# Half-height score products, one hidden pair moved into the round before, and a causal mask split in three, in a two-layer recurrent kernel

## The reference

```python
xn = _layernorm(x)
s = _L0_attn_ref(xn, ...)          # tanh mixes, r k v w g, wkv6, group norm, W_o
g = _silu(_L0_ffn_ref(xn, ...))    # silu(gate)*up, 2-of-4 sparsity, down
x = x + s * g
xn = _layernorm(x)
s = _L1_attn_ref(xn, ...)          # _ssd, below, times silu(res), w_out
g = _silu(_L1_ffn_ref(xn, ...))
x = x + s * g
```

```python
L = jnp.where(tri, jnp.exp(cs[..., :, None] - cs[..., None, :]), 0.0)
scores = jnp.einsum('znid,znjd->znij', Cc, Bc) * L
y_diag = jnp.einsum('znij,znjh->znih', scores, Xc)
```

## Time and profile before

| | us |
|---|---|
| median of 3 runs (lowest, highest) | 735.85 (734.74, 736.4) |
| the profiled execution | 735.66 |
| its span, first to last instruction | 733.9 |
| TensorE busy in the span (matmuls) | 711.3 (97%) |
| VectorE, ScalarE, GpSimd busy | 497.5, 342.0, 77.2 |
| chain that ended last: TensorE, VectorE, issue | 76%, 12%, 5% |

### The profile page before, as it was taken

The page is one execution under the profiler, slowest core; times in us unless marked ns, Lnnn a source line. Parts: engine busy times, 40 slices in busy tenths (PEclk is TensorE's granted clock), DMA queues, the critical chain, the costliest instruction groups (busy, mean ns, idle before and its releaser), DMA issues.

```text
span 733.9 us, 17949 instructions
## 1 busy us (share of the span) xinstructions
PE 711.3 (97%) x6896; PEld 590.1 (80%) x6896; DVE 497.5 (68%) x1207; ACT 342.0 (47%) x678; POOL 77.2 (11%) x85
## 2 busy tenths in 40 slices
PE   5998999999999999999999999999999999999998
PEld 3777688877888688886888868888788878888686
DVE  4976599547895478955787558855689547895133
ACT  1411685226832468215762168522584236821690
POOL 6301011101011010100111001110101101011020
PEclk9989999999999999999999999999999999999999
DMA  7900351125400353013531145102540136301360
GB/s 238 404 23 29 102 88 32 15 73 144 75 2 15 88 146 59 2 28 104 117 59 16 30 138 95 32 15 69 142 80 3 15 87 145 59 2 26 119 116 16
DMA packets 122444, 55.93 MB, mean 76 GB/s; under 512 B 104384, under 2 KB 114176, under 8 KB 120832
## 3 DMA queue, kind: packets, MB, share of 16 engines
q1 hardware_dynamic: 122368, 54.76, 30.3%
HBM read 42.35 MB, written 12.40 MB: 75 GB/s over the span
## 4 chain that ended last, share of the span: by engine, by line
PE 76%; DVE 12%; issue 5%; DMA 2%; SPq 2%; ACT 2%; POOL 1%; DVEq 0%; ACTq 0%; POOLq 0%
PE psum L1486 58%; PE psum L1707 2%; PE psum L1722 2%; PE psum L1514 2%; PE psum L1565 1%; PE psum L1760 1%; PE psum L1931 1%; PE psum L1595 1%; PE psum L1733 1%; DVE beats L1085 1%; PE psum L1577 1%; DVE own L992 1%; PE psum L1554 1%; PE psum L1873 1%; SPq L453 1%
## 5 line engine op out<-in xcount | busy, mean ns | idle before, releaser
L602 ACT ACTIVATE BC<-psum 64x256 f32<-64x256 f32 x128 | 81.4, 636 | 3.0 <-PE psum L1486 1.3
L1486 PE MATMUL psum<-xn1T,sb_n_gate 128*128 128x256 f32 x256 | 61.3, 382 | 0.0
L1486 PE MATMUL psum<-xn1T,sb_n_up 128*128 128x256 f32 x256 | 60.6, 380 | 0.4 <-DVE cs_row L1294 0.4
L1486 PE MATMUL psum<-xnT,sb_f_gate 128*128 128x256 f32 x240 | 58.5, 386 | 0.0
L1486 PE MATMUL psum<-xnT,sb_f_up 128*128 128x256 f32 x240 | 57.6, 382 | 0.0
L733 ACT ACTIVATE thFB<-psum 128x512 f32<-128x512 f32 x8 | 4.8, 597 | 104.9 <-PE psum L1486 104.9
L1486 PEld LDWEIGHTS psum<-xn1T,sb_n_up 128*128 128x128 f32 x256 | 48.0, 190 | 6.9 <-DVE cs_row L1294 0.8
L1486 PEld LDWEIGHTS psum<-xn1T,sb_n_gate 128*128 128x128 f32 x256 | 48.0, 190 | 6.8
L1486 PEld LDWEIGHTS psum<-xnT,sb_f_up 128*128 128x128 f32 x240 | 44.8, 190 | 6.4 <-issue 0.3
L1486 PEld LDWEIGHTS psum<-xnT,sb_f_gate 128*128 128x128 f32 x240 | 44.2, 189 | 6.8 <-issue 0.2
L1486 PE MATMUL psum<-sb_f_down,hid 128*128 128x256 f32 x224 | 49.5, 379 | 0.0
(11 more groups left out here) (257 smaller groups left out, 1459.0 us busy)
## 6 DMA issues: line engine op xcount, KB each, us to landing
cs_row<-cs_dram SPq DMA_DIRECT2D x8, 1024.0 KB, 4.9
x_dram<-gate SPq DMA_DIRECT2D x8, 512.0 KB, 2.8
cs_half<-cs_dram SPq DMA_DIRECT2D x16, 256.0 KB, 5.9
hidB<-x_dram SPq DMA_DIRECT2D x8, 512.0 KB, 5.9
b_dram<-B_turned SPq DMA_DIRECT2D x32, 128.0 KB, 3.3
hidB<-b_dram SPq DMA_DIRECT2D x8, 512.0 KB, 4.2
X<-in_x SPq DMA_DIRECT2D x9, 256.0 KB, 3.5
XT<-in_x_turned SPq DMA_DIRECT2D x8, 256.0 KB, 3.6
```

The costliest lines, as they stand in the source:

```text
L602: ins = a_.activation(cols[:, par, 2 * pair:2 * pair + 2, :], src[64 * par:64 * par + 64, :, s, :], ACT.Identity)
L1486: ins = t_.matmul(ps(t, name)[first_row:first_row + rows, col:col + n], w, x, start=(k == 0), stop=(k == len(ws) - 1))
```

## The change

1. **Scores by 64 keys.** Each product of 128 keys with 128 queries becomes two of 64 keys: the first 64 keys with all 128 queries, the last 64 keys with the last 64 queries. They stand in the two column halves of the array and swap sides from chunk to chunk. The keys of odd chunks thus lie with their halves exchanged, so `cs_pos`, `Xrow` and `Brow` are loaded by three DMAs each (`KEY_ROWS`).
2. **Mask in three.** Even chunks, odd chunks, and the lower 64 partitions of the odd chunks have a select each, one behind the other; where there is a tile a they wait for `lev_ready` 4, the last of the four `level_next` before `own_taken`.
3. **Pair 1 at the end of the round before**, behind pair 0, in other banks; `th` is filled there by silu (`next_gates`), `hidden_p(a, 1)` stands behind `hidden_p(a, 0)`, and all of `compare(0)` before `mix_g_scaled`.
4. **Order elsewhere.** `end_args` behind `B_by_block`, `gate_tanh` behind `L_exps(0)`, `res0` before `gate_in`; in round 0 the down product is cut up around `keys_turned` and `chunk_states`, the fillers become 4 and 9 products of 128 columns and the last one goes; in round 8 the first B product stands before `carries`.

```diff
+KEY_ROWS = [(slice(0, P), 0, slice(0, P)), (slice(0, 64), 1, slice(64, P)), (slice(64, P), 1, slice(0, 64))]
...
-            return name not in ("p0", "p1", "p2") or (name == "p2" and t.first) or (name == "p0" and not t.first)
+            return name not in ("p0", "p1", "p2") or t.first == (name == "p2")
...
-                    sp_.dma_start(Brow.rearrange("p q c d -> p (q c) d"),
-                                  b_dram.rearrange("(c p d) -> p c d", p=P, d=SD)).then_inc(B_rows, 16)
+                    keys = b_dram.rearrange("(c two p d) -> p c two d", two=2, p=P, d=SD)
+                    for to, r, from_ in KEY_ROWS:
+                        sp_.dma_start(Brow.rearrange("p q (c two) d -> p (q c) two d", two=2)[to, :, r, :],
+                                      keys[from_, :, r, :]).then_inc(B_rows, 16)
...
-                    g.affine_select(out=cs_row[:, :, :], in_=cs_row[:, :, :], compare_op=ALU.is_ge, fill=NEG, base=0,
-                                    pattern=[[0, NQ * SCH], [1, P]], channel_multiplier=-1).then_inc(cs_masked, 1)
+                    if a:
+                        pool.wait_ge(lev_ready, a.count(6, 4))
+                        pool.sem_inc(passed, 1)
+
+                    by_two = cs_row[:, :, :].rearrange("p (c two) q -> p c two q", two=2)
+                    for last, r, two, base in ((P, slice(0, P), 0, 0), (P, slice(0, P), 1, 64), (64, slice(0, 64), 1, -64)):
+                        m = by_two[r, :, two, :]
+                        ins = g.affine_select(out=m, in_=m, compare_op=ALU.is_ge, fill=NEG, base=base,
+                                              pattern=[[0, NQ * SCH // 2], [1, P]], channel_multiplier=-1)
+                        if last == P:
+                            did(ins)
+                    ins.then_inc(cs_masked, 1)
...
-                    for s in range(NQ):
-                        r = half_rows(s)
-                        ins[s] = t_.matmul(ps(t, names[s])[:, i * P:(i + 1) * P], Bf[r, c * P:(c + 1) * P],
-                                           Cf[r, c * P:(c + 1) * P], start=True, stop=True)
+                    for first in range(2):
+
+                        k, at = slice(c * P + 64 * first, c * P + 64 * first + 64), 64 * (first ^ (c % 2))
+                        for s in range(NQ):
+                            r = half_rows(s)
+                            ins[s] = t_.matmul(ps(t, names[s])[at:at + 64, i * P + 64 * first:(i + 1) * P], Bf[r, k],
+                                               Cf[r, c * P + 64 * first:(c + 1) * P], start=True, stop=True)
...
-                    kept_at_work("p2u", 1)
+                    kept_at_work("p2u", 4)
...
-                    down_part(a, 0, 0, 4)
+                    down_part(a, 0, 0, 2)
+                    keys_turned()
+                    down_part(a, 0, 2, 4)
+                    chunk_states()
+                    down_part(a, 1, 0, 2)
                     outputs()
-                    down_part(a, 1, 0, 4)
-                    kept_at_work("yT", 1)
+                    down_part(a, 1, 2, 4)
+                    kept_at_work("yT", 9)
...
-                    kept_at_work("xT1", 6)
+                    ffn_p(a.next(), 1)
```

More of the change, by code:

```diff
@@ L103, in place @@
         b = BANK[name]
-        return b, self.count(PER[b], NTH[name] + EXTRA[b])
+        behind = 2 if name in ("p1g", "p1u") else 0
+        return b, self.count(PER[b], NTH[name] + EXTRA[b] - behind * PER[b])
     def at(self):
@@ L427, in one @@
                     sp_.sem_inc(passed, 1)
-                    wait(X_rows, b.count(16, 16))
+                    wait(X_rows, b.count(48, 16))
                     sp_.dma_start(x_dram.rearrange("(q p n) -> p q n", q=NQ, p=P), Xnat).then_inc(X_stored, 16)
@@ L432, in one @@
                     sp_.sem_inc(passed, 1)
-                    wait(cs_loaded, b.count(48, 16))
+                    wait(cs_loaded, b.count(80, 16))
                     wait(cs_rows_loaded, b.count(16, 16))
@@ L444, in one @@
                     wait(X_stored, b.count(16, 32))
-                    sp_.dma_start(Xrow.rearrange("p q c d -> p (q c) d"),
-                                  x_dram.rearrange("(c p d) -> p c d", p=P, d=SD)).then_inc(X_rows, 16)
-                    wait(B_rows, b.count(16, 16))
+                    keys = x_dram.rearrange("(c two p d) -> p c two d", two=2, p=P, d=SD)
+                    for to, r, from_ in KEY_ROWS:
+                        sp_.dma_start(Xrow.rearrange("p q (c two) d -> p (q c) two d", two=2)[to, :, r, :],
+                                      keys[from_, :, r, :]).then_inc(X_rows, 16)
+                    wait(B_rows, b.count(48, 16))
                     wait(B_blocks, b.count(2, 2))
@@ L733, in ffn_tanh_1, with next_gates @@
                     free(a_.activation(thFB[:, :], ps(b, "F1")[:, :], ACT.Silu, scale=0.5), b, "F1")
+                def next_gates():
+                    for n in range(2):
+                        ffn_tanh(a.next(), f"p{n}", th[n], None)
+                    exp_tables()
                 def exp_tables():
@@ L782, in one @@
                     ffn_tanh_1()
+                    if a.reg is not None:
+                        next_gates()
                 elif a:
@@ L898, in hidden @@
                     return
-                dve.wait_ge(ready, t.count(2, n + 1 if t.first else n))
+                dve.wait_ge(ready, n + 1 if t.first else t.count(1, 2))
                 free(d.scalar_tensor_tensor(out=buf[:, :], in0=buf[:, :], scalar=1.0, in1=ps(t, name + "g")[:, :],
@@ L1124, in differences, with rank_inputs @@
                 did(d.tensor_tensor(dxT[:, :, :], xnT[:, :, 0:T], xnT[:, :, 1:T + 1], ALU.subtract))
+            def rank_inputs(t):
                 after()
@@ L1334, in one @@
                     hidden_p(a, 0)
+                    hidden_p(a, 1)
                     mix_scaled(a, "w")
@@ L1357, in one @@
                     own_taken(a)
-                    end_args()
                     B_by_block(0)
                     B_by_block(1)
+                    end_args()
                     level_next(a, 4)
@@ L1397, in one @@
                     differences(a.next())
+                    rank_inputs(a.next())
                     result()
@@ L1465, in _ @@
             differences(Tile(None, 0, first=True))
+            rank_inputs(Tile(None, 0, first=True))
             rounds(dve, one)
@@ L1902, in kept_at_work @@
                     for _ in range(count):
-                        t_.matmul(ps(a, name)[:, 0:C], ident[:, :], W["f_gate"][:, 0:C], start=True, stop=True)
+                        t_.matmul(ps(a, name)[:, 0:P], ident[:, :], W["f_gate"][:, 0:P], start=True, stop=True)
                 def turned_1():
@@ L1975, in one @@
                     low_levels(a)
+                    ssd_proj(b, "res0", "w_res", 0)
                     gate_in()
-                    ssd_proj(b, "res0", "w_res", 0)
                     ssd_proj(b, "res1", "w_res", 1)
@@ L2069, in one @@
                     X1()
+                    ssd_proj(b, "B0", "w_B", 0)
                     carries()
-                    for name, w in (("B", "w_B"), ("C", "w_C")):
-                        for half in range(2):
-                            ssd_proj(b, f"{name}{half}", w, half)
+                    ssd_proj(b, "B1", "w_B", 1)
+                    for half in range(2):
+                        ssd_proj(b, f"C{half}", "w_C", half)
                     ffn_n(b, 0)
```

49 lines of the change are left out of this document (22 added, 27 removed).

## The result

| | before | changed |
|---|---|---|
| median of 5 runs (lowest, highest), us | 735.15 (734.74, 736.4) | 739.99 (737.96, 741.55) |
| ratio, 95% interval | | 1.0068 (1.0049 to 1.0088) |
| the profiled execution, its span | 735.66, 733.9 | 741.55, 739.8 |
| mean clock in the profiled execution | 0.995 | 0.998 |

The change makes the kernel slower by 0.7%. I had forecast 725.5, faster, with 0.08 for slower; both the sign and the size are wrong. The profiled execution is the slowest of the five: TensorE's clock fell in its round 5. Three of the others have a mean clock of 1.0 and take 737.96 to 739.99.

The account below looks back on a forecast made before the run. The prediction took TensorE's stream, busy 91.60 of 92.00 us in a steady stretch, as the bound. From 735.66 us, -2.8 - 4.1 - 0.6 - 3.4 + 0.8 = -10.1 gave 725.5 us, range 722.5 to 732.0.

Parts of the forecast that it names:

- 0.08 for slower: Whole kernel: the chance given to the change making it slower, against 0.88 for faster and 0.04 for same.
- My part on pair 1: Steady rounds: 3.55 us only moved, costing nothing; between rounds 0 and 1 a gain, -3.55 - 0.6 = -4.1 us.
- the mask's term: Before the high levels: mask behind level 4 makes them later, net 0.2 us a round, bounds -0.2 and +0.5.
- My slower rival: Mask: each select costs what the whole one does, 2.6 us later a round, 744 us; chance 0.05.
- Scores: Scores by 64 keys: 1.48 us instead of 1.99, saving 0.51 us a round.
- the fixed cost: Rival on the scores: a cost per product eats most of the 0.51 us, 728.5 us; chance 0.06.
- quarters in turn: Rival on the scores: array quarters don't run side by side, 3.0 us instead of 1.48, 736 us; chance 0.04.
- the mask's move in round 1: Round 1: the mask no longer blocks a VectorE comparison, a gain of some 0.6 us, between 0 and 1.8.
- The forecast clock: Round 0: longer first filler keeps TensorE's clock up, worth 3.4 us; rival that it falls, 729 us, chance 0.30.
- my 0.6 for the cut-up down product: Round 0: the pieces fill earlier waits, so the chain behind the outputs comes 0.6 us sooner.
- +0.8: Round 8: the end hangs on Brow, whose added DMA issues make it 0.8 us later, bounds 0 and 3.
- What I said would make it wrong: A steady round not about 0.3 us shorter, or a gain of rounds 0 and 1 under 4 us.

Follow-up runs that it names:

- e1: The changed kernel with TensorE's loop beginning at the first slot of a 16 KB instruction block (head_slot 0): 730.9 us, ratio to before 0.9939.
- e7: The kernel before with TensorE's loop at the first slot of a block (head_slot 0), nothing else: 731.94 us, ratio 0.9978.
- e6: The kernel before with only the scores by 64 keys, the mask in three selects and end_args behind the transposes: 738.83 us, ratio 1.0055.
- e13: The kernel before with the loop at the first slot and the three edits of VectorE's order from e12: 730.17 us, ratio 0.9947.
- e2: The kernel before with TensorE's loop at slot 220 of 256 (head_slot 220): 744.79 us, ratio 1.0154.
- e12: e1 with low_taken before level 6's copies, e8's smaller select, and decayed_scores(0) and states_0 (rounds 1 to 7) and round 8's scores before B_decayed: 719.94 us.
- e3: A run with the hint; the text given states neither its kernel nor its time.
- e4: The changed kernel with GpSimd's three selects no longer waiting for level 4: 762.2 us, ratio 1.0389.
- e14: The kernel of e12 with TensorE's loop left where the changed kernel has it: 733.88 us, ratio 0.9985.
- e9: The changed kernel with TensorE's loop at slot 205 of 256 (head_slot 205): 732.66 us, ratio 0.9964.
- e8: e1 with the second select cut to the 64 partitions and 64 queries that need it: 727.56 us, ratio 0.9902.

## Why the prediction was wrong

My sum was -10.1, measured were +5.9 in the profiled execution. Of the 16 us between them, 14.7 lie in rounds 2 to 6.

- **The step that failed first: what is done to the code in front of the loop costs a steady round nothing.** My part on pair 1 said that in a steady round its 3.55 us "are only moved" and "I cost it at nothing". It followed the moved products' waits, but not their instructions: round 0 has more code in front of the loop, and that shifts the loop in its blocks. It cost 8.9 us of pauses, some 1.7 of clock in round 5 and 0.5 before the rounds' first product. No rival named it; none of my views of the kernel before showed it, since there was no pause there, but the profile's line of instruction packets and the branch back were both to be seen.
- **It is not all of it.** With the pause gone a steady round of e1 is still 0.6 us longer than that of its control e7, where I had forecast 0.3 shorter. Most of these 0.9 us is the mask's term, next; the rest I can't split.
- **Mask: the mechanism was right, the term mis-sized.** I had net +0.2 a round, bounds -0.2 and +0.5, and measured +0.81 in round 3, 0.7 to 0.8 in the others. The selects took 1.1 us each, as I said. Two other sizes were off. The starts: I gave the mask 3.4 us behind level 4's last copy, with 0.1 for the two waits between the selects; it took 276.33 - 272.46 = 3.87, since 0.6 us went by before and between the selects. So level 5 was late by 0.70 and not by 0.4. The slack: I counted the 0.39 us from the banks' freeing to the high levels before (283.89 to 284.28) as slack, and let TensorE start 0.2 us behind the freeing. With TensorE waiting there it starts 281.62 - 281.18 = 0.44 us behind it, so there was none. My slower rival had each select cost 2.0 us; the selects did not (1.09), so it was right only in where the lateness goes, to the high levels.
- **Scores: right.** 1.48 forecast, 1.50 measured; the rivals of the fixed cost and of quarters in turn are out.
- **Pair 1: the size was right, the round wrong.** I booked -3.55 in round 1. But round 1 makes pair 1 for round 2 at its own end; the one that falls away is round 7's. Put there, my sum has -5.5 for rounds 0 and 1 and -3.05 for 7 and 8; measured were -4.4 and -2.9. The wait of 0.67 us in round 1 went as forecast. Of the 0.6 for the mask's move in round 1 nearly 0.5 came: its way from the low to the high levels was 10.14 us against 9.46 in round 3, and is 10.50 against 10.28.
- **Round 0.** The forecast clock held: none of the eleven profiled executions with the changed round 0 has a fall in it, and four of the five with before's round 0 do (before, e6, e7, e13). But the 3.4 us were the size of the fall in one execution of before; in e6, e7 and e13 it is half as long, 1.7 us, and before's mean clock in most other executions was 0.998 or 1.0. e2, whose round 0 is before's own, kept the clock as well and reached round 1 at 68.41, sooner than the changed kernel at 69.05. So the difference of 3.42 is the clock, and my 0.6 for the cut-up down product did not show.
- **Round 8.** +0.8 was too little: the scores' wait grew from 0.35 to 1.6 us, to 2.4 in e1, hidden in the total by the pair.
- **What I said would make it wrong** (a steady round not 0.3 us shorter, less than 4 us from rounds 0 and 1): the first happened; rounds 0 and 1 gave 4.4. With the loop's place and the waits mended, e12 against e13 gives -10.2. That this is nearly my -10.1 is in part luck: rounds 2 to 6 gave 1.8 against 1.55 in my sum, but rounds 0 and 1 gave 4.4 against 5.5, and rounds 7 and 8 gave 5.0 against 3.05.

## What to carry to other kernels

In a loop whose body is longer than a fetch block, as here, code ahead of the loop is part of its timing: fix the loop's place (or give the branch's hint) before comparing two versions, count the instruction packets of both, and suspect the place when an engine pauses "for issue" at the same instruction of every pass but the first. When a step is taken out from before a chain, look for what used to be over by then, as the mask here, and for what on the same engine now waits in front of work that doesn't need it: here these reorderings and the smaller select took the kernel from 730.9 (e1) to 719.94 us (e12). And a saving in a loop that only moves work to the pass before is booked in the last pass, not the first.

## What the runs showed of the hardware

- In every run but e3 (the hint), e7 and e13, a 16 KB block of its program was on its way 0.4 to 1.2 us behind the start of rounds 2 to 6. Where TensorE paused for it (the changed kernel, e2, e4, e14), execution went on 2.3 to 2.8 us after that fetch began. With the loop's head about 36 instructions short of a block's end TensorE paused 1.1 to 1.7 us by the waits; at 51 short (e9) `X0` took up to 0.25 us more.
- A loop of 1802 TensorE records a pass fetched 9 blocks a pass at its old place and none in rounds 2 to 6 with its head at slot 0 (e7, e13: 21 packets in all against 66). One of 1864 records fetched 10 a pass at its old place and 9 at slot 0 (e1).
- Twice a pause of 1.66 us was followed by a lower clock: `X0` took 3.26 and 3.60 us instead of 1.98, while four other rounds of e2 had as long a pause (3.66 to 3.70 us to `X0`) and kept it.
- GpSimd's select takes its time by elements per partition: 1.09 us for 1024 on 128 partitions, 1.08 for 1024 on 64, 2.01 for 2048, 0.66 for 512 on 64 (e8). While it runs, VectorE's copy of 128x256 within SBUF took 1.18 us instead of 0.28 (e4), and an operation on 16 columns 0.90 instead of 0.17.
